# A gated cross-attention and FFN kernel on one core: transposes of the next rows set singly between matmuls, and two block products of the last slice exchanged

## The reference, cut to what matters

```python
def _layernorm(x, axis=-1, eps=1e-05):
    m = jnp.mean(x, axis=axis, keepdims=True)
    v = jnp.var(x, axis=axis, keepdims=True)
    return (x - m) / jnp.sqrt(v + eps)
...
    x = x + jnp.tanh(g_xattn[0]) * _L0_xattn_ref(_layernorm(x, axis=-1), ctx_1024, ctx_1024, Wq, Wk, Wv, Wo)
    x = x + jnp.tanh(g_ffn[0]) * _L0_ffn_ref(_layernorm(x, axis=-1), w_gate, w_up, w_down)
    return x
...
    # _L0_xattn_ref: 16 heads of 32; softmax(q k^T * 32^-0.5, causal), times v, then Wo
    # _L0_ffn_ref: integer weights over 127, hidden width 1536
        gate = jnp.einsum('bsd,hd->bsh', x, wg)
        up = jnp.einsum('bsd,hd->bsh', x, wu)
        h = jax.nn.silu(gate) * up
        return jnp.einsum('bsh,dh->bsd', h, wd)
```

## Time and profile before

| | us |
|---|---|
| median of three runs | 873.64 (873.36 to 874.93) |
| the profiled execution, device time | 874.07 |
| its span, first to last instruction | 872.3 |
| PE busy | 855.0 (98%) |
| DVE, ACT, POOL busy | 652.8, 460.5, 402.3 |

### The profile page before, as it was taken

How to read it: one execution, slowest core, us unless ns; L and a number is a source line. 1 busy time by engine, 2 the same in 40 slices (tenths; PEclk the granted TensorE clock), 3 DMA queues, 4 the chain that set the end, 5 groups by cost and what they waited for, 6 DMA issues and landing times.

```text
span 872.3 us, 12869 instructions
## 1 busy us (share of the span) xinstructions
PE 855.0 (98%) x4087; PEld 707.9 (81%) x4087; DVE 652.8 (75%) x1081; ACT 460.5 (53%) x1130; POOL 402.3 (46%) x344
## 2 busy tenths in 40 slices
PE   8999999999999999999999999999999999999997
PEld 7678888888888887788888888888888888888876
DVE  5988877778786877679688478788487877587882
ACT  5687575666666757446056264165362364460550
POOL 4665555556564664437144444155253255251350
PEclk9999999999999999999999999999999999999999
DMA  9233847272728131567333256043265143243302
GB/s 334 73 109 118 276 152 248 84 240 93 233 97 277 68 113 51 198 235 265 115 123 133 96 190 249 12 165 121 79 248 182 47 164 113 96 166 116 97 31 98
DMA packets 60406, 128.73 MB, mean 148 GB/s; under 512 B 7616, under 2 KB 20416, under 8 KB 60352
## 3 DMA queue, kind: packets, MB, share of 16 engines
q1 hardware_dynamic: 58960, 125.95, 41.7%
q10 hardware_dynamic: 1392, 2.10, 0.7%
HBM read 99.93 MB, written 27.79 MB: 146 GB/s over the span
## 4 chain that ended last, share of the span: by engine, by line
PE 87%; DVE 6%; ACT 3%; issue 1%; DMA 1%; POOL 1%; ACTq 0%; DVEq 0%
PE psum L1814 34%; PE psum L1548 29%; PE psum L1864 18%; PE psum L1573 4%; DMA gates<-g_ffn 1%; PE psum L1657 1%; ACT e L791 1%; POOL hT L696 1%; DVE bn L1034 1%; DVE e L1076 1%; DVE K L1128 1%; DVE mx L1073 1%; DVE qT L1058 0%; DVE pT L1047 0%; DVE aT L1058 0%
## 5 line engine op out<-in xcount | busy, mean ns | idle before, releaser
L1814 PE MATMUL psum<-xv,ring 128*128 128x512 f32 x1344 | 308.2, 390 | 0.9 <-ACT a L964 0.7
L1814 PEld LDWEIGHTS psum<-xv,ring 128*128 128x128 f32 x1344 | 251.5, 188 | 55.1 <-ACT a L964 1.1
L696 POOL TENSOR_TENSOR hT<-th,hT 128x512 fp32r<-128x512 f32 x48 | 86.3, 1798 | 201.2 <-ACT hT L984 201.2
L1864 PE MATMUL psum<-w_d,hT 128*128 128x512 f32 x768 | 177.7, 391 | 1.3 <-POOL hT L696 0.8
L1864 PEld LDWEIGHTS psum<-w_d,hT 128*128 128x128 f32 x768 | 143.7, 188 | 32.6 <-POOL hT L696 2.0
L554 POOL TENSOR_TENSOR e<-e,rden 128x616 f32<-128x616 f32 x64 | 77.9, 1217 | 110.4 <-DVE rden L1110 73.8
L791 ACT ACTIVATE e<-psum,nmx,q_scale 128x77 f32<-128x77 f32 x256 | 102.6, 427 | 2.3 <-DVE nmx L1090 2.2
L952 ACT ACTIVATE a<-psum 128x512 f32<-128x512 f32 x48 | 28.7, 599 | 131.7 <-PE psum L1814 131.4
L1428 DVE SCALAR_TENSOR_TENSOR acc<-psum,gate_ffn,acc 128x512 f32<-128x512 f32 x64 | 47.7, 750 | 65.1 <-PE psum L1864 65.1
L1548 PE MATMUL psum<-wo,aT 128*128 128x512 f32 x384 | 95.2, 399 | 0.5 <-DVE aT L1058 0.5
L1548 PE MATMUL psum<-xT,wq 128*128 128x512 f32 x360 | 89.0, 398 | 0.4 <-DVE qT L1058 0.4
(11 more groups left out here) (110 smaller groups left out, 1204.6 us busy)
## 6 DMA issues: line engine op xcount, KB each, us to landing
ring<-w_var SPq DMA_DIRECT2D x48, 896.0 KB, 4.6
w_var<-stage SPq DMA_DIRECT2D x12, 896.0 KB, 4.6
x_ln<-x SPq DMA_DIRECT2D x32, 256.0 KB, 4.6
x_res<-x SPq DMA_DIRECT2D x32, 256.0 KB, 5.0
x_mid<-x_res SPq DMA_DIRECT2D x32, 256.0 KB, 2.0
x<-x_mid SPq DMA_DIRECT2D x16, 512.0 KB, 5.6
acc<-x_mid SPq DMA_DIRECT2D x16, 512.0 KB, 6.4
out<-acc SPq DMA_DIRECT2D x32, 256.0 KB, 2.0
```

The lines of the kernel that those rows point to most:

```text
L696: nc.gpsimd.tensor_tensor(hT[:, 1, i % HH, j, :], h[:, :], hT[:, 0, i % HH, j, :].bitcast(f32), ALU.subtract).then_inc(h_lo, 1)
L1814: last = nc.tensor.matmul(psum[:, bank, :], stat, mov, start=start and j == 0, stop=j == len(terms) - 1, skip_group_check=not start)
L1864: last = nc.tensor.matmul(m_bank[t % 2][:, :], hT[:, a, m, t // TT, (t % TT) * P:(t % TT + 1) * P], w_d[:, HH * h + m, :], start=m == 0 an ...
```

## The change: what it does

On TensorE the groups of 8 transposes are taken apart. A transpose now stands behind each of the first matmuls of a product: B11 and B12 between the matmuls of `down(p, 1, 0)` and `down(p, 1, 1)`, B22 between those of `down(p, 1, 2)`, B21 between those of `down(p, 1, 3)`. For the first pair, B22 and B21 go between the matmuls of the third and fourth V product. What a group waits for now stands ahead of the product that carries it. In slice 11 `p7` goes ahead of `p5`. The last slice's wait for its low part stands behind 16 matmuls of down products where it stood behind 20. ACT and DVE take up the moved pieces in another order.

```diff
@@ ACT, end of a pair @@
+                tanh2(last)
+                tanh1(last)
+                h_high(last, 0)
                 if more:
                     xv_copy(p + 1, B11, b11_at)
-                tanh2(last)
-                tanh1(last)
+                h_high(last, 1)
                 if more:
                     b12_copy(p + 1)
-                h_high(last, 0)
-                h_high(last, 1)
-                if more:
                     xv_high(p + 1, T1)
@@ DVE, last V products @@
                 m_low(H_LAST + m + 1, m, aT[:, 1, m, :], aT[:, 0, m, :])
-                if m == 1:
-                    form(0, T2)
-                if m == 2:
-                    form(0, T3)
+            form(0, T2)
+            form(0, T3)
+            residual(NB, 0)
             xv_low(0, B21, b21_at)
-            residual(NB, 0)
+            residual(NB, 1)
             form(0, T4)
-            residual(NB, 1)
+            residual(NB, 2)
             xv_low(0, B22, b22_at)
-            residual(NB, 2)
             residual(NB, 3)
@@ DVE, end of a pair @@
                 silu2(last)
-                if more:
-                    xv_low(p + 1, B11, b11_at)
                 silu1(last)
...
                 if more:
+                    xv_low(p + 1, B11, b11_at)
+                result(p, 1, 0)
+                if more:
                     form(p + 1, T1)
-                result(p, 1, 0)
                 result(p, 1, 1)
@@ TensorE @@
-            def product(dst, terms):
+            def product(dst, terms, after=None):
                 for j, (stat, mov) in enumerate(terms):
                     last = nc.tensor.matmul(dst, stat, mov, start=(j == 0), stop=(j == len(terms) - 1))
+                    if after is not None:
+                        after(j)
...
+            def turning(q, j):
+
+                at = turn_ready(q, j)
+
+                def after(i):
+                    if i < KH * TT:
+                        turn_x(j, at, i)
+                return after
...
-            for m in range(G):
-                values(M_LAST + m, m, B - 1, T_P2 - 2 + min(m, 2))
-                if m == 1:
-                    turn(0, B22)
-            turn(0, B21)
+            values(M_LAST, 0, B - 1, T_P2 - 2)
+            values(M_LAST + 1, 1, B - 1, T_P2 - 1)
+            values(M_LAST + 2, 2, B - 1, T_P2, turning(0, B22))
+            values(M_LAST + 3, 3, B - 1, T_P2, turning(0, B21))
...
-                    p5(i)
-                    p7(i)
+                    if m == MH - 1:
+                        p7(i)
+                        p5(i)
+                    else:
+                        p5(i)
+                        p7(i)
...
-                if more:
-                    turn(p + 1, B11)
-                    turn(p + 1, B12)
                 p4(last)
                 p3(last)
-                down(p, 1, 0, range(HH - 1))
-                down(p, 1, 1, range(HH - 1))
+                if more:
+                    first_k, second_k = turning(p + 1, B11), turning(p + 1, B12)
+                    down(p, 1, 0, range(HH - 1), lambda i: first_k(i) if i < KH * TT else second_k(i - KH * TT))
+                    down(p, 1, 1, range(HH // 2), lambda i: second_k(i + 2 * (HH - 1) - KH * TT))
+                else:
+                    down(p, 1, 0, range(HH - 1))
+                    down(p, 1, 1, range(HH // 2))
...
                 down(p, 1, 0, range(HH - 1, HH))
-                down(p, 1, 1, range(HH - 1, HH))
+                down(p, 1, 1, range(HH // 2, HH))
                 if more:
-                    turn(p + 1, B22)
-                    turn(p + 1, B21)
-                for t in range(2, PT):
+                    down(p, 1, 2, range(HH), turning(p + 1, B22))
+                    down(p, 1, 3, range(HH), turning(p + 1, B21))
+                for t in range(4 if more else 2, PT):
                     down(p, 1, t)
```

## The result

The changed kernel takes 879.49 us (median of 4 runs, 878.78 to 879.67), the kernel before 873.50 beside it (4 runs, 873.31 to 874.93). The ratio is 1.0064, with a 95% interval of 1.0052 to 1.0077: slower by 6.0 us, where 6.4 were forecast. The profiled execution took 879.56 us with a span of 877.8, which is 5.5 more than the span before.

A forecast was written before the change was run, and what follows sets the result against it. TensorE, busy 98% of the span, was taken to bound the kernel. Three pairs at 1.8 us (5.4), plus 1.1 at attention's end, less 0.1 in the last pair, gave 6.4 us: 880.0, range 875.2 to 883.0 (8 in 10).

The forecast's parts named there:

- Step 1: Pair's end, before p4: with the covering transposes gone, TensorE waits 0.3 us for snapshot a3 and starts again.
- Step 2: 16 matmuls of down(1, 0) and down(1, 1) with 16 lone transposes at 0.125 us each: 5.65 us.
- Step 3: TensorE's wait for POOL's low part goes, removing 0.42 + 0.14 us; POOL's chain ends near 723.6, TensorE comes 1.1 later.
- Steps 4 and 5: 8 matmuls, down(1, 2) with 8 transposes to 730.27, then down(1, 3); B21 is turned 5 us later, last transpose 732.97.
- Step 6: result(1, 3) comes 4.42 us behind B21's last transpose, so down(1, 5) waits 0.64 us, plus 0.14 for restarting.
- Step 7: result(1, 4), on DVE behind xv_low(B22), comes at 740.65; down(1, 6) waits 0.38 us, plus 0.14 for restarting.
- Step 8: Last 24 matmuls and the start end the pair at 746.26 against 744.49: 1.8 us later for each of three pairs.
- End of attention: The projection, waiting for the last V result without the 8 transposes filling the wait, starts at 362.47, 1.1 us later.
- Last pair: p4 may start about 0.4 us sooner, but p3 waits for c22 behind DVE's search in both kernels: -0.1 us.
- the waits for results don't come: Rival: no waits before down(1, 5) and down(1, 6); a pair costs 0.5 us, in all 2.5: 876.1. Chance 0.10.
- Only its columns: Rival: a lone transpose between matmuls costs 0.065 us; the sum is about 1 us, 874.6. Chance 0.08.
- vanish: Rival: the 112 lone transposes hide between matmuls at 0.014 us each; sum -2.3 us, 871.3. Chance 0.07.

The follow-up runs named there:

- run without the swap: Changed kernel with DVE taking result(p, 1, 3) and result(p, 1, 4) earlier, and p5 ahead of p7 again in slice 11: 876.51 us, ratio 1.0034.
- order-only kernel: Kernel before, TensorE untouched, with ACT and DVE in the changed order at a pair's end (T1 still ahead of result(p, 1, 0)): 871.82 us, ratio 0.9981.
- V-products kernel: Kernel before with only the end of attention changed, B22 and B21 transposes between V-product matmuls and DVE's order there: 874.32 us, ratio 1.0009.
- results-first kernel: Changed kernel, but DVE takes result(p, 1, 3) ahead of B21's xv_low and form T4, and result(p, 1, 4) ahead of B22's xv_low: 875.10 us, ratio 1.0017.
- swap alone: Kernel before with p7 ahead of p5 in slice 11 of each pair, nothing else: 873.79 us, ratio 1.0000.
- order-and-swap kernel: The order-only kernel with p7 ahead of p5 in slice 11 added: 872.20 us, ratio 0.9986 to the kernel before.
- kernel with the search moved: The order-and-swap kernel, with DVE's largest-weight search in the last pair's last slice moved behind hidden1: 871.96 us, ratio 0.9980 to the kernel before.

## Why the prediction was right

880.0 was forecast and 879.49 measured. By its steps, for a pair (1.8 forecast, 1.6 measured):

- **Step 1, the wait for a3.** The snapshot started at 720.68, right behind L984 at 720.15, as forecast. TensorE's starts are 0.47 us apart there, 0.24 over a matmul, where 0.3 was forecast. The run without the swap, with 1.07, shows that it is this wait.
- **Step 2, the lone transpose.** The term was mis-sized. 0.125 us was taken; seven periods from 734.56 to 736.98 are 0.346 each, less 0.228 for the matmul is 0.118. The two kernels that differ in how the transposes stand give 0.010 over a block's 0.108, the same. On 32 transposes this is 0.2 us a pair, and with it the pair's forecast falls from 1.8 to 1.6: nearly the whole of the miss.
- **Step 3, POOL.** The wait went, as forecast. Its slack was put at 1.1 us and is 0.4: POOL ends at 728.34, and the product that needed it is the first of the nine from 728.73 on. POOL is through 5.2 us behind the end of p3's matmuls (721.32 + 8 x 0.228 = 723.14), where 4.5 were summed (719.06 to 723.6). Two terms were missing, of opposite sign. DVE's silu2 (L1389) took 1.66 us in that chain where it took 0.69 before (the last section). And ACT no longer has B11's copy ahead of tanh2, which then starts 1.46 us behind the snapshot (722.14 and 720.68) in place of 1.92 (718.91 and 716.99). That the error cost nothing is luck: 0.4 us more of it would have brought the wait back.
- **Steps 4 and 5.** down(1, 2) and down(1, 3) ran on; B21's last transpose started 4.44 us ahead of down(1, 5), where 4.42 was summed.
- **Step 6.** The first wait for a result is 0.92 us from start to start, so 0.69 over a matmul; 0.64 was forecast.
- **Step 7.** The second: B21's last transpose to down(1, 6) 7.70 us, forecast 732.97 to 740.65, which is 7.68. Its starts are 0.60 apart (744.08 to 744.68), 0.37 over a matmul; 0.38 was forecast.
- **Step 8.** Added from the measured parts: 0.3 for the transposes, 0.24 + 0.69 + 0.37 for the waits, -0.42 for POOL's, and two more restarts at 0.12, which is 1.4 of 1.6. About 0.1 more stands ahead of p4; the forecast named p7 behind p3, at 0.1, and left it out of the 1.8. It is this: the row at 719.12 shows p7's weight loads released by a2, and the two order-only kernels, with and without the swap, differ by 0.09 a pair. The kernels also add up step by step. A pair takes 123.5 us with the order alone; 123.9 with the groups moved behind p3 and the swap, where the wait for a3 and p7's for a2 appear; 124.2 with the FFN transposes set singly; 125.6 with the results behind B21 and B22. The kernel before has 124.0, its wait for POOL included.
- **End of attention.** 1.0 measured, in the changed kernel and alone; 1.1 forecast. The cheaper transposes took 0.1 off, and the 1.89 in place of 1.81 us behind the last V matmul gave it back in part.
- **Last pair.** -0.3, forecast -0.1. p3 does wait for c22 behind the search and starts when it did, as said: 98.45 us behind the pair's start, 98.46 before. The gain lies behind it: the wait of 0.50 us for the first result is gone, and one of 0.28 for POOL stands in its place, -0.24 up to the last result. The rest is not the change's. What follows the last result differs from trace to trace: the V-products kernel, whose last pair is that of the kernel before, takes 126.9 us from its start to the end of the span, not 127.65.

Of the rivals, "the waits for results don't come" is refuted by the rows, and the results-first kernel shows what it would have been worth: 1.3 us over the kernel before, where the rival gave 2.5, with a transpose cheaper by 0.007 (0.8 over 112) and the last pair by 0.2 as most of the difference. "Only its columns" (0.065) and "vanish" (0.014) are refuted by 0.118, "dearer" (0.158) as well. Two numbers of these rivals don't fit the rest of the prediction: they have POOL hold TensorE until 723.95, where step 3 has it done near 723.6, and the fixed part in rows 3 is 0.010 to 0.013 (0.141 less 308 columns, 0.2277 less 512), not 0.014. Neither bears on the forecast. The Trainium skill's rule from "TensorE: Matmul & The Clock Gate", section "LDWEIGHTS (loading the stationary operand)", agrees with the block's 0.108. The prediction's reading of it beside a matmul, that the load of the transpose is covered and then that of the matmul behind it is not, agrees with 0.118; no run tests it by itself. The timeline shows the matmul behind each lone transpose with 0.48 us of its own where one in a run has 0.39.

What the forecast had not seen is that the change holds a gain. It reckoned the removed wait for POOL at -0.56 a pair but left it inside a sum that came out slow; the order-only kernel shows that this term comes from ACT's and DVE's order and needs none of TensorE's edits.

## What to carry to other kernels

Transposes threaded singly between matmuls cost here what they cost in a block and 0.01 us more; what decides is where the last of them ends, because everything behind it in an in-order queue is late by as much. Before a producer is moved later, go down the queue of the engine that consumes it, and look for an instruction that is not concerned but stands behind it (here a result that frees a bank); taking that one first gave back 1.4 of the 1.6 us that a pair had lost. And take a change that comes out slow apart by engine: here ACT's and DVE's order at the pair's end alone was worth -0.2%, while the whole came out at +0.6%.

## What the hardware did that was not expected

DVE's silu2 reads two tiles of SBUF. Where it overlaps POOL's L696 it ends 0.55 us after POOL does, whenever it began:

| kernel | DVE starts, takes | POOL ends | DVE ends after |
|---|---|---|---|
| changed | 722.81, 1.66 | 723.91 | 0.56 |
| swap alone | 719.90, 0.73 | 720.08 | 0.55 |
| without swap | 721.28, 1.19 | 721.93 | 0.54 |
| order only | 717.49, 1.18 | 718.12 | 0.55 |

These are the third pair's last slices. The same holds all through: in each of the ten traces 39 or 40 of the 48 instructions of this kind start while POOL still runs, and they end 0.54 to 0.57 us after it. Where nothing of POOL is beside it, it takes 0.69 us (in the last pair of the order-and-swap kernel, at 842.22). It looks as if DVE stood still until POOL was done and did nearly all of its work then. The Trainium skill says this of the two engines ("SBUF — State Buffer", section "Who interferes with whom"): they share a pair of ports under an exclusive lock, and an instruction of DVE that needs both its inputs from SBUF is held while GpSimd has it. The four rows agree. The 1.0 us more that silu2 took (1.66 less 0.69) is more than the 0.7 missing from the slack in step 3; tanh2's earlier start gave 0.46 back. So a slack on DVE beside POOL's work is to be counted from POOL's end.

POOL is held up by DVE as well. Its low part (L696, `hT<-th,hT`) takes about 1.8 us nearly everywhere, and nearly everywhere DVE's hidden2 (`c<-c,th`, two tiles of SBUF) has begun 0.04 us before it. In the last slice of the kernel with the search moved, hidden2 comes later, and POOL takes 1.29:

```profile
844.73 1.29 POOL L696 TENSOR_TENSOR hT<-th,hT 128x512 fp32r<-128x512 f32 x1 [2.62 <-ACT hT L984]
```

In the kernel before, this half microsecond lies in the chain that TensorE waits for at the end of each pair (723.46, 1.81). That another place for hidden2 would take that wait away too is an estimate from these rows; no run tries it.
